# Attention set-up of a gated cross-attention block: loads of K's inputs ahead of x's tiles, and V's projection dealt out anew on TensorE

## The reference

```python
# x: (2, 2048, 512), ctx: (2, 77, 512), 16 heads of 32
n = layernorm(x)                                   # over the last axis
q = n @ Wq.T + bq;  k = ctx @ Wk.T + bk;  v = ctx @ Wv.T + bv
attn = softmax(q k^T / sqrt(32)) per head          # 77 keys
x = x + tanh(g_xattn) * ((attn @ v) @ Wo.T + bo)
h = gelu(qlinear(layernorm(x), w1, b1))            # both factors rounded to 127 steps
x = x + tanh(g_ffn) * qlinear(h, w2, b2)
```

## Time and profile before

| what | value |
| --- | --- |
| median of 3 executions | 601.37 us (600.62 to 601.69) |
| the profiled execution's own time | 602.49 us |
| its span | 600.7 us (so 1.8 us lie around it) |
| TensorE busy | 577.6 us, 96% of the span |
| VectorE busy | 452.5 us, 75% |
| ScalarE busy | 336.4 us, 56% |
| GpSimd busy | 251.2 us, 42% |
| mean DMA rate | 177 GB/s |

### The profile page before, as it was taken

One profiled execution on the slowest core, in us unless ns is written; L12 is line 12 of the kernel. 1 busy time (PEld: TensorE's weight loads), 2 busy tenths in 40 slices (PEclk: granted clock), 3 DMA queues, 4 the chain that ended last, 5 costly groups with the idle time before them and its releaser, 6 DMA issues. The chain is left out here.

```text
span 600.7 us, 9216 instructions
## 1 busy us (share of the span) xinstructions
PE 577.6 (96%) x3288; PEld 326.4 (54%) x3288; DVE 452.5 (75%) x645; ACT 336.4 (56%) x408; POOL 251.2 (42%) x218
## 2 busy tenths in 40 slices
PE   7799899999999999999999999999999999999997
PEld 3653656747557566575674774444444454444443
DVE  3585895977959878686795687989998789944282
ACT  3236364483772845637437545878776678544440
POOL 4447546574565663926054410000004519223373
PEclk9989979999999999999999999999999999999999
DMA  8944111140410503202001139777777967788776
GB/s 308 391 171 139 73 37 35 53 160 0 167 45 7 186 19 106 106 0 107 1 1 71 70 143 393 293 282 288 265 278 298 420 221 285 276 353 337 234 268 210
DMA packets 41815, 106.62 MB, mean 177 GB/s; under 512 B 3248, under 2 KB 4016, under 8 KB 37168
## 3 DMA queue, kind: packets, MB, share of 16 engines
q1 hardware_dynamic: 39824, 103.70, 46.6%
q10 hardware_dynamic: 1952, 2.42, 1.3%
HBM read 64.16 MB, written 41.94 MB: 177 GB/s over the span
## 5 line engine op out<-in xcount | busy, mean ns | idle before, releaser
L1456 PE MATMUL ps<-h_sb,w_q 128*128 (+1 forms) x488 | 109.8, 379 | 1.5 <-ACT xo L1523 1.5
L1755 PE MATMUL ps<-w_q,h_q 128*128 128x512 bf16 x448 | 96.9, 379 | 0.0
L1838 POOL TENSOR_TENSOR xo<-xo,b2s 128x512 f32<-128x512 f32 x32 | 52.5, 1674 | 70.1 <-DMA xo<-x_dram 52.1
L1456 PEld LDWEIGHTS ps<-h_sb,w_q 128*128 128x128 bf16 x488 | 46.6, 98 | 53.8 <-ACT xo L1523 2.8
L1755 PEld LDWEIGHTS ps<-w_q,h_q 128*128 128x128 bf16 x448 | 43.8, 98 | 52.9
L1523 ACT ACTIVATE xo<-ps,b1s,sc 128x1024 f32<-128x1024 f32 x48 | 57.6, 1205 | 24.6 <-PE ps L1456 20.7
L743 ACT ACTIVATE prob<-ps 77x1024 f32<-77x1024 f32 x64 | 61.6, 1013 | 12.9 <-PE ps L489 12.8
L729 ACT ACTIVATE q_hi<-ps,bq_sb 128x512 fp32r<-128x512 f32 x32 | 22.0, 688 | 80.9 <-DVE ps L938 80.9
L1623 DVE TENSOR_REDUCE hmax<-xo 128x1024 f32 (+1 forms) x48 | 57.1, 1213 | 5.7 <-ACT xo L1523 5.6
L1173 POOL TENSOR_TENSOR xt_lo<-xr,xt_hi 128x512 fp32r<-128x512 f32 x28 | 35.5, 1290 | 46.6 <-ACT xt_hi L725 46.4
L1815 DVE SCALAR_TENSOR_TENSOR xo<-ps,hs,xo 128x512 f32<-128x512 f32 x32 | 23.3, 746 | 40.0 <-POOL xo L1838 39.5
(11 more groups left out here) (185 smaller groups left out, 1135.8 us busy)
## 6 DMA issues: line engine op xcount, KB each, us to landing
h_dram<-xo SPq DMA_DIRECT2D x48, 512.0 KB, 2.7
h_sb<-h_dram SPq DMA_DIRECT2D x16, 1024.0 KB, 11.1
x_dram<-x SPq DMA_DIRECT2D x8, 1024.0 KB, 3.8
xo<-x_dram SPq DMA_DIRECT2D x8, 1024.0 KB, 5.0
x<-h_dram SPq DMA_DIRECT2D x8, 1024.0 KB, 8.2
x<-in_x SPq DMA_DIRECT2D x7, 1024.0 KB, 7.3
xr<-in_x_t SPq DMA_DIRECT2D x28, 256.0 KB, 3.0
out<-xo SPq DMA_DIRECT2D x7, 1024.0 KB, 7.6
```

The source lines that it names most:

```text
L1456: mm = nc.tensor.matmul(ps[:, 2 * (m % 2) + s, :], w1_q[:, k, m * P:(m + 1) * P], xq_t[:, one(2 * j + s), k, :], start=(k == 0), stop=(k = ...
L1755: mm = nc.tensor.matmul(ps[:, 4 * s + t, :], h_q[s][:, m, t * P:(t + 1) * P], w2_q[:, m, :], start=(m == 0), stop=(m == MF - 1))
L1838: nc.gpsimd.tensor_tensor(xo[:, s, t, :], xo[:, s, t, :], b2s[:], ALU.add).then_inc(xb_on, 1)
```

## The change

Five edits. On SyncE the load of the first half of wk goes ahead of two of x's four tiles of chunk 0. On ScalarE the loads of the context and of the second half of wk go ahead of x's other two tiles. On SyncE `load_x(2)` goes ahead of `load_xt(1, 2)`, with K's wait alone; `load_x(3)` keeps V's. On TensorE the third q tile is finished ahead of the first scores by token, the fourth directly behind them, and V's eight quarters are dealt out anew. On VectorE `stats1` gets a second wait, on VectorE's own earlier aggregates.

```diff
@@ SyncE
                 for k in (0, 2):
                     sp.dma_start(xt0_raw[:, k, :], xt_v[k, 0]).then_inc(xt0_in[k], 16)
+                sp.dma_start(wk_raw[:, 0:2, :], slices(wk_t)[:, 0:2, :]).then_inc(k_in, 16)
                 for t in (0, 2):
                     sp.dma_start(x1[:, t, :], x_v[0][:, t, :]).then_inc(x0_in[t], 16)
-                sp.dma_start(wk_raw[:, 0:2, :], slices(wk_t)[:, 0:2, :]).then_inc(k_in, 16)
...
+                sp.wait_ge(k_biased, GROUPS)
+                load_x(2)
                 load_xt(1, 2)
                 load_xt(1, 3)
-                sp.wait_ge(k_biased, GROUPS)
                 sp.wait_ge(v_on, B)
-                load_x(2)
                 load_x(3)
@@ TensorE, first_step
                     first_q(1, [2, 3])
+                    first_q(2, [2, 3])
                     pe.wait_ge(k_split_hi, 4)
                     scores_by_token(0, 0)
-                    first_q(2, [2, 3])
-                    project_v(0, range(KD // 4))
+                    first_q(3, [2, 3])
+                    project_v(0, range(0, 1))
                     scores_by_token(0, 1)
-                    first_q(3, [2, 3])
-                    project_v(0, range(KD // 4, KD // 2))
+                    project_v(0, range(1, 3))
                     scores_by_token(0, 2)
-                    project_v(0, range(KD // 2, KD))
+                    project_v(0, range(3, KD))
+                    project_v(1, range(0, 1))
                     scores_by_token(0, 3)
-                    project_v(1, range(3 * KD // 4))
+                    project_v(1, range(1, 2))
                     transpose_max(0)
...
                     scores_by_key(0, 0)
-                    project_v(1, range(3 * KD // 4, KD))
+                    project_v(1, range(2, KD))
@@ ScalarE, its loads
+                nc.scalar.dma_start(ctx_sb, slices(ctx_t)).then_inc(k_in, 16)
+                nc.scalar.dma_start(wk_raw[:, 2:4, :], slices(wk_t)[:, 2:4, :]).then_inc(k_in, 16)
                 for t in (1, 3):
                     nc.scalar.dma_start(x1[:, t, :], x_v[0][:, t, :]).then_inc(x0_in[t], 16)
-                nc.scalar.dma_start(ctx_sb, slices(ctx_t)).then_inc(k_in, 16)
-                nc.scalar.dma_start(wk_raw[:, 2:4, :], slices(wk_t)[:, 2:4, :]).then_inc(k_in, 16)
@@ VectorE, stats1
                     dve.wait_ge(x_in, 16 * c)
+                    dve.wait_ge(ln1_aggr, TT * c)
```

## The result

The changed kernel takes 597.94 us (median of 20, 596.04 to 599.26) against 601.23 us (median of 20) for the kernel before: a ratio of 0.9950, 95% interval 0.9938 to 0.9963, or 3.0 us less by the ratio (3.3 by the two medians). The prediction said 596.9 in a range of 594.3 to 599.8, and faster with 0.87. It was faster, and inside the range; the gain by the ratio was two thirds of the 4.5 us forecast.

What follows compares the result with a forecast made beforehand. TensorE, busy 96%, was the bound, so only its waits or low clock could give time. Transposes 4.4 plus chunk 2's x 0.34 made 4.75 us (596.6 from the median); weighed against 598.2 at full clock it took 596.9, range 594.3 to 599.8.

Steps and rivals of the forecast that it cites:

- K's loads: Set-up: wk lands at about 16.9 instead of 20.2, so TensorE's 1.46 us wait before K's projection goes.
- x's tiles late: Chunk 0: x's own tiles land at about 20.2, hidden behind K's projection with some 1.3 us to spare.
- Third q tile: Before the first scores by token: fills 1.37 of TensorE's 1.81 us wait, leaves 0.44, scores not delayed.
- From the scores to the transposes: Chunk 0: V dealt anew leaves VectorE's cycle as bound; transposes at 37.6 instead of 42.00, 4.4 us sooner including K's 1.46.
- the other case: Chunk 0 without the low clock at 31 us before: old transposes at 40.4, gain 2.8 + 0.34 = 3.2 us, or 598.2.
- Two quarters of V behind the scores by key: Chunk 0: they take 1.72 us, end at 41.0 before the exponentials release TensorE at 41.5; cost 0.
- Chunk 2's x: Chunk 1: sooner load removes VectorE's 6.78 us wait and TensorE's 0.34 us; counted 0.34, bounds 0 and 2.7.
- The low clock in chunk 1: Rival, 18%: the low clock at 75 us in chunk 1 shrinks too, 2.5 us to be had, 594.4.

Runs made afterwards that it cites:

- e8_q_ahead: Changed kernel with V's quarters back in their old places, third q tile still ahead of the first scores by token; 599.22 us, one execution.
- e9_v_dealt: Changed kernel with the q tiles back in their old places, V still dealt out anew; 598.64 us, one execution.
- b1_before: The kernel before, unedited, run once more for its trace; 598.63 us.
- e1_loads: Kernel before with only the loads reordered, wk and the context ahead of x's tiles; 598.20 us, ratio 0.9953 to the kernel before.
- e3_x2: Kernel before with only chunk 2's x asked for sooner; 600.01 us, ratio 0.9988 to the kernel before.
- e6_x3_late: Changed kernel with the load of x's chunk 3 held until ScalarE has copied chunk 1's transposed tiles; 598.12 us, one execution.
- e2_tensor: Kernel before with only TensorE's order changed, third q tile ahead and V dealt anew; 599.39 us, ratio 0.9970 to the kernel before.
- e4_undo_loads: Changed kernel with wk and the context again behind x's tiles; 599.25 us, ratio 0.9976 to the kernel before.
- e5_turns: Changed kernel with 9 and 12 idle transposes in chunk 1's two TensorE waits; 596.18 us, ratio 0.9934 to the kernel before.
- e7_both: Changed kernel with idle transposes in chunk 1's two TensorE waits and chunk 3's load held back; 595.81 us, ratio 0.9914 to the kernel before.

## Why the prediction was right, and where its size was off

**K's loads: 1.46 us, right as a mean, wrong as a constant.** Five traces of the old order give q - K of 7.11 to 9.48, on average 8.07, against 6.57: 1.5 us. On the transfer itself: wk's second half landed at 19.1 to 20.4 in the five traces of the old order (issue plus time to landing) and at 16.4 to 17.6 in the nine of the new one, 3.0 us sooner on average. I had taken 3.3 by bytes, an estimate from the queue's rate. The measured time is near it, but doesn't confirm it: ScalarE's issue also came 1.5 us sooner (4.2 to 4.3 against 5.3 to 6.2), which the reckoning doesn't have. The queues shared the engines: in the 3 us of the earlier trace rows, where ScalarE's took 46.5% of their span, SyncE's took 57.4%, and from 24 to 30 us SyncE's, alone, took 105%. The sum rests on the wait of 1.46 us, not on the 3.3.

**x's tiles late: right.** Hidden; a wait of 0.32 us on VectorE, none on TensorE.

**Third q tile: right.** In the trace of before the mark of 1.81 us at 29.12 names K's high parts, but ScalarE had ended these at 28.31 and ended q's first high tile at 29.03: the tile was what ended last, and the releaser in the mark was its neighbour. 0.44 us of the 1.81 stays, in every trace with it, and the scores aren't delayed. What I didn't see is that it gives nothing without V's new places, and they nothing without it (e8_q_ahead, e9_v_dealt).

**From the scores to the transposes: the term that was mis-sized.** I set 4.4 us for the transposes as a whole, of which 1.46 were K's: some 2.9 for this stretch. In the pair of traces it was 12.88 - 10.33 = 2.55, but 12.88 - 11.26 = 1.6 of that is the low clock at 31 us, which lasted some 3.4 us. Of the five traces with a wait of 1.81 us there (before, b1_before, e1_loads, e3_x2, e9_v_dealt) only the one that I read has it. At full clock the step is worth 11.26 - 10.33 = 0.93. The prediction had the other case, 3.2 us and 598.2, and gave it the smaller weight, though the median of before lay 1.1 us below its profiled execution. That the range still held the result owes something to this: the forecast of 596.9 was a weighted mean of two cases, and the measured 597.94 is next to the case that it gave less weight. What decides whether the low clock comes isn't shown. A second, smaller miss of 0.4 us is in the same term. I let the fourth `token_max` start when `q_low` was through, at 8.5 us behind the first `q_low`; it started at 35.54 - 26.65 = 8.9, since the scores that it reads begin at 34.70, which is 0.23 behind the fourth `q_low`, and extend over 0.81 us, where I had let them begin with `q_low` and used 0.63, the distance to the next matmul.

**Two quarters of V behind the scores by key: right.** No cost; 0.29 us of idle time is left.

**Chunk 2's x: right for the wrong sum.** The wait of 6.78 us went. The 0.34 us that I counted isn't there in b1_before nor in e1_loads, and against it stand marks of 0 to 0.7 us for the last transposed tile, which came in with TensorE's order and went when chunk 3's load was held back (e6_x3_late). I had written that the transposed tiles keep their own later wait, and did not ask what comes behind them on the queue. The worth of the edit is another: with TensorE's new order alone, the old place costs 1.2 us in the one trace (e2_tensor), and with the new place that wait is gone (e4_undo_loads).

**The low clock in chunk 1: the rival didn't come as such.** It took 5.1 us in all traces of the changed kernel and 3.8 or 6.5 in those of before. Where it took 6.3 to 6.5, the hidden stage took 105 us, and where 5.1, 107. What a trace gains at one it gives back at the other; only the kernels with idle transposes have the lower value at both (b1_before and e9_v_dealt, with 3.8, have 106.7 and 106.8 again). These 1.2 to 2.1 us of the hidden stage go with low clock too. About 21 us into that stage TensorE waits for ScalarE's `xo` in every trace. Here are the profile after and e5_turns, with the same wait of 2.27 us, and between them the clock in the profile after:

```profile
366.31 3.07 PE L1458 MATMUL ps<-h_sb,w_q 128*128 128x512 bf16 x8 [2.27 <-ACT xo L1525]
```

```profile
368.00:369.00 1.00, 1.00 (x4) 0.50 0.97 367
```

```profile
366.42 1.90 PE L1463 MATMUL ps<-h_sb,w_q 128*128 128x512 bf16 x8 [2.27 <-ACT xo L1530]
```

In the eight traces with 106.6 to 107.0 us the clock is 0.50 behind this wait. In the six with 104.9 to 105.4 it isn't: before, e3_x2 and e8_q_ahead have their low clock at the start of the stage instead, where it doesn't show in the length, and e4_undo_loads, e5_turns and e7_both have none. Why this goes with the length of the low clock in chunk 1 isn't shown. Of the 2.2 us that the pair of traces seemed to give back, 1.2 (106.6 - 105.4) are this, and not the change's doing: b1_before has 106.7 as well. The other 1.0 comes behind the last landmark. From there to the end the nine traces with the reordered loads take 144.0 to 144.7 us, the five others 143.5 to 144.0, on average 0.6 more with the loads, for which I have no reason.

Summed from the traces: 1.5 + 0.1 for K, 0.93 to the transposes, less some 0.3 for the last transposed tile and 0.6 at the end, is 1.6 us. Measured were 3.0, 4.2 and 3.1. K's long waits with their low clock (1.7 us in one of five traces) and the clock at 31 us (1.6 in one of five) add about 0.3 each; the mean clocks give the same, as an estimate: 0.9928 in 60 executions of before and 0.9940 in 38 of the changed kernel are 1.5 us less at 0.50, worth 0.7 at most (3.4 us at 0.50 cost 1.6 from the scores to the transposes in the trace of before, and 1.7 from K's projection to the scores in e2_tensor). That makes 2.3 us, beside the 2.6 to 3.7 on which the three comparisons agree. What is left, 0.3 to 1.4 us, I can't place.

## What to carry to other kernels

A single profiled execution can hold a stretch of low clock that most executions don't have (here 1.6 us in one trace of five): before its time goes into a sum, compare the profiled time with the median and work the sum out a second time at full clock. Where two engines hand work to and fro, count both: an edit on one gives only what the other's cycle leaves, and two edits that are worthless alone can be worth more together (0.93 us here). When one engine gets ahead, look also at the small loads that it will now ask for sooner, and at what large load stands right behind them in the queue (marks of 0 to 0.74 us here, gone in the two traces with the load held back).

## What the runs showed of the hardware

- After a TensorE wait of 1.81 us the granted clock fell to 0.50 in one of five traces; after one of 2.75 us it fell in the one trace that has it, as K's projection had begun, and was back at 1.00 by 25 us.
- Where it was 0.50 for 3.4 us, the work took 1.6 us longer (from the first scores to the transposes, before against b1_before) and 1.7 us longer (from K's projection to the scores, e2_tensor against before).
- At chunk 1's waits of 1.22 and 1.54 us it fell in ten of twelve traces. With nine and twelve idle transposes in these waits it stayed at 1.00 in both traces that have them.
- Behind the hidden stage's wait for `xo` it fell in eight traces. After a wait of the same 2.27 us it fell in the profile after and not in e5_turns. The stage took 1.2 to 2.1 us longer where it fell.
- The landing of the same 512 KB transfer, with the same work ahead of it, varied from 19.1 to 20.4 us between executions. The start of q varied too (10.90 to 12.18 us in the same five), and the wait for the transfer from 0.39 to 2.75 us.
- From 9 to 12 us in the trace of before SyncE's queue took 57.4% of the DMA engines' span and ScalarE's 46.5%; from 24 to 30 us SyncE's alone took 105%.
